# Moving elementwise steps between three engines in a five-pass graph network: low parts to GpSimd, normalisation to ScalarE, the last graph pass's own projection to ScalarE with its bias as a matmul

## Chip, cores and metric

One NeuronCore of a Trainium2 chip runs the whole program. The metric is the device time of one execution in microseconds (us); each kernel is executed several times and the median is given.

The engines are named as the profile names them: PE is TensorE's matrix unit and PEld its weight load, DVE is VectorE, ACT is ScalarE, POOL is GpSimd, SP is SyncE, which here only issues DMAs.

## What is computed

`x` holds 128 graphs of 64 nodes with 384 features, `adj` a weighted 64x64 adjacency for each. Four layers follow one another, each as `x = layernorm(x + layer(x, adj))`, all in fp32:

```
L0, L3: q, k, v = x@Wq.T, x@Wk.T, x@Wv.T + bv      (12 heads of 32)
        p = softmax(q k^T * scale + edge * adj)
        out = (p v) @ Wo.T + bo
L1:     the same with biases on q and k, beta*adj added, p masked
        where adj is 0, and no output projection
L2:     two inner layers, each
        a = softmax(h h^T / sqrt(384)); delta = a * adj
        attn = delta / (sum(delta) + 1e-10)
        ctx = (attn above diag) @ (h Wl.T + bl) + diag(attn) * (h Ws.T + bs)
              + (attn below diag) @ (h Wr.T + br)
        h = relu(layernorm(ctx) * g + b)
```

## The kernel before

The program is five passes over the same 8192 rows, one behind the other, with a barrier between them and the rows kept in device memory from pass to pass: `attention_pass` for L0 and L1, `digcn_pass` for the two inner layers of L2 (called the first and the last graph pass here), `attention_pass` for L3. The last graph pass has `ends` true: it also adds the residual and makes the outer layernorm. L0 and L3 have an output projection (`wo` true), L1 has none.

A pass treats 16 groups of 512 rows. A group is 4 units (s = 0 to 3) of 128 rows, two graphs each, so that a pass has 64 units. Every engine has its own program for a pass, written out by hand as `group(i, pair, par)`, which `over_groups` repeats; the engines meet only through semaphores, and each works through its queue strictly in order. The order of work is therefore exactly the order in which the calls stand in the five `group` functions.

**Precision by parts.** Projections multiply fp32 values as a rounded high part plus a low part. For rows, DVE turns a tile of 128x512 (`rows_turned`, L717), ACT copies it rounded into `xT[..,0,..]` (`rows_high`, L584), and the difference goes into `xT[..,1,..]` (`rows_low`): in L0 and L3 on DVE at the tail of units 2 and 3 (L723), in L1 on POOL at the tail of the same units (L372). Each projection is then 9 matmuls, in three combinations of parts. A pass does the three tiles of a group two groups ahead (attention) or one to two ahead (graph passes).

**An attention unit.** PE makes scores (L471), DVE scales them and adds the edge bias (`softmax_max`, L751), takes the row maximum (L758) and in L0 and L3 the minimum (L760). POOL subtracts the maximum (L387) and adds the bias of v for the unit (`value_bias`, L347). ACT exponentiates (L656). DVE sums (L765) and makes the reciprocal (L770 to L776). In L0 and L3 POOL adds `bo` to the residual rows (L355) and multiplies the probabilities (L398), PE transposes them (L484), the next unit but one multiplies them with v (L509), ACT and DVE split that product into parts (`oT`: L666 and `low_part`, L798), and PE makes the output projection (`output`, L524). DVE adds the residual (`residual`, L807), takes mean and variance (L811, L814), POOL makes the reciprocal root (`rstd`, L339 and L341), and DVE's `normed` writes the normalised rows (L823, one 128x384 instruction), which SP stores. In L1 POOL adds the residual (`add_rows`, L366).

Between these, PE makes the projections of the next group, ten blocks (q, k, v: L450, L444) put between the steps of the four units by the table `BETWEEN`; ACT copies each block out of PSUM (`taken`: q L598/L596, k L605/L602, v L615).

**A graph unit.** PE projects the rows left, right and self (`project`, L1165, 9 matmuls each) and, between right and self, multiplies the unit before with its attention (`context`, L1179). In unit 1 `products` (L1138) follows that, in unit 3 `attention_T` (L1149) stands behind self. ACT copies left and right out (L1242), POOL adds their biases (L1092). DVE's `itself` adds the own bias to the self projection (`hs`, L1386), `context` makes `c0 = hs * diag + ps_c` with its statistics (L1398, L1401, L1404), `inner_norm` scales, shifts, adds the residual and takes the second statistics (L1412 to L1425). In the last graph pass ACT standardises (L1259) and writes the final rows (L1267). DVE's own order in a graph unit is `itself`, `rows_turned` (L1332, units 0, 2, 3), attention steps 3 and 4 in unit 3 (L1366 to L1379: the normalised attention `wide`, which `attention_T` waits for, and `diag`), `inner_norm`, `context`, and at the tail attention step 0 (unit 1) or steps 1 and 2 (unit 2: L1352 to L1361).

## Time and profile before

| | |
|---|---|
| median of 3 executions | 2729.84 us (2726.38 to 2730.54) |
| the profiled execution, its own time | 2732.55 us |
| its span, first to last instruction | 2730.8 us |
| busy in the span: PE, DVE, POOL, ACT | 90%, 83%, 69%, 53% |
| mean granted TensorE clock | 0.966 of 2.4 GHz |
| first instruction queued by each pass: L0, L1, graph 1, graph 2, L3 | about 8, 646, 1192, 1607, 2095 us |

A row of the timeline reads: start and duration in us, engine, line, operation, output<-inputs (buffer numbers left out), shapes, xcount for merged neighbours, and in brackets the idle time ahead of it with what ended it. The windows view gives, for a stretch, the busy time of each engine with its number of instructions, then the granted clock as a share of 2.4 GHz. A busy share is an average: what bounds a stretch is read from the waits and from which engine never waits.

### The profile page before, as it was taken

To read this page: it belongs to the slowest core of one execution; us is meant where nothing else is said; L and a number is where in the kernel's file an instruction comes from. 1 tells how busy PE (TensorE), PEld (TensorE's weight loads), DVE (VectorE), ACT (ScalarE), POOL (GpSimd) and SP (SyncE) were. 2 spreads that over 40 slices of the span, in tenths; PEclk is the share of its full clock that TensorE was granted. 3 is DMA by queue.
4 is the path that set the end of the run, shared out by engine and by line. 5 is a ranking of instruction groups with operands and counts; after the bars stand their busy time and mean duration, and the time that the engine had idled before them with its cause. 6 is when DMAs were issued, how large, how long until landed. Compare 5 with 4: busy or idle time off the path is not lost. (4 is left out here: it accounts for less than half of the span.)

```text
span 2730.8 us, 64297 instructions
## 1 busy us (share of the span) xinstructions
PE 2468.6 (90%) x21490; PEld 2094.7 (77%) x21490; DVE 2263.7 (83%) x3822; ACT 1456.9 (53%) x2964; POOL 1895.4 (69%) x2093
## 2 busy tenths in 40 slices
PE   6999999995999999959999978998895999999997
PEld 5888888874877777748888867777774788888886
DVE  5999999984788888867777769889897699999997
ACT  4555555552666666535544545555554555555553
POOL 2777777773677777756666647788784577777776
PEclk9999999997999999979999989999997999999999
DMA  7222222115233332163332163333324222222211
GB/s 133 62 66 70 70 66 70 47 46 104 63 80 76 90 76 66 54 125 72 73 67 64 50 114 83 89 91 76 92 65 95 49 66 70 67 68 70 58 45 51
DMA packets 320740, 200.89 MB, mean 74 GB/s; under 512 B 243440, under 2 KB 320624, under 8 KB 320624
## 3 DMA queue, kind: packets, MB, share of 16 engines
q1 hardware_dynamic: 320624, 199.40, 31.6%
q8 instruction: 66, 1.08, 0.2%
q14 instruction: 50, 0.41, 0.0%
HBM read 136.42 MB, written 62.91 MB: 73 GB/s over the span
## 5 line engine op out<-in xcount | busy, mean ns | idle before, releaser
L450 PE MATMUL l_ps_p<-l_xT,l_w 128*128 128x512 f32 x2304 | 602.7, 409 | 99.6 <-POOL l_xT L372 50.4
L1165 PE MATMUL l_ps_h<-l_w,l_hT 128*128 128x384 f32 x3456 | 658.1, 345 | 10.1 <-DVE l_hs L1386 7.3
L1165 PEld LDWEIGHTS l_ps_h<-l_w,l_hT 128*128 128x128 f32 x3456 | 607.1, 191 | 74.0 <-issue 42.4
L450 PEld LDWEIGHTS l_ps_p<-l_xT,l_w 128*128 128x128 f32 x2304 | 430.9, 193 | 197.1 <-issue 102.2
L387 POOL TENSOR_TENSOR l_pr<-l_sc,l_st 128x768 f32<-128x768 f32 x192 | 283.1, 1475 | 328.8 <-DVE l_st L758 327.6
L347 POOL TENSOR_TENSOR v<-v,l_bvs 128x768 f32<-128x768 f32 x192 | 375.6, 1956 | 0.0
L1242 ACT ACTIVATE l_hlr<-l_ps_h 64x384 f32<-64x384 f32 x512 | 248.8, 486 | 228.3 <-PE l_ps_h L1165 219.1
L1092 POOL TENSOR_TENSOR l_hlr<-l_hlr,l_sides 128x768 f32<-128x768 f32 x128 | 240.1, 1876 | 119.9 <-ACT l_hlr L1242 119.9
L444 PE MATMUL l_ps_p<-l_w,l_xT 128*128 128x384 f32 x1584 | 311.2, 342 | 0.0
L615 ACT ACTIVATE v<-l_ps_p 64x192 f32<-64x192 f32 x704 | 228.6, 325 | 142.0 <-PE l_ps_p L444 135.3
L765 DVE TENSOR_REDUCE l_st<-l_pr 128x12 f32<-128x768 f32 x192 | 182.7, 952 | 126.9 <-ACT l_pr L656 125.7
L524 PE MATMUL l_ps_y<-l_w,l_oT 128*128 128x384 f32 x1152 | 237.6, 352 | 47.2 <-DVE l_oT L798 43.5
L444 PEld LDWEIGHTS l_ps_p<-l_w,l_xT 128*128 128x128 f32 x1584 | 273.1, 188 | 5.8 <-issue 0.2
L524 PEld LDWEIGHTS l_ps_y<-l_w,l_oT 128*128 128x128 f32 x1152 | 204.6, 193 | 80.9 <-issue 77.3
L398 POOL TENSOR_TENSOR l_pr<-l_pr,l_st 128x768 f32<-128x768 f32 x128 | 211.1, 1649 | 38.0 <-DVE l_st L776 28.6
L656 ACT ACTIVATE l_pr<-l_pr 128x768 f32<-128x768 f32 x192 | 163.1, 850 | 85.4 <-POOL l_pr L387 81.4
L751 DVE SCALAR_TENSOR_TENSOR l_sc<-l_ps_s,l_sbias 128x768 f32<-128x768 f32 x192 | 183.6, 956 | 30.1 <-PE l_ps_s L471 22.3
L651 ACT ACTIVATE l_pT<-l_ps_t 128x512 f32<-128x512 f32 (+1 forms) x384 | 167.5, 490 | 50.0 <-PE l_ps_t L484 44.4
L758 DVE TENSOR_REDUCE l_st<-l_sc 128x12 f32<-128x768 f32 x192 | 183.0, 953 | 6.7
L605 ACT ACTIVATE l_k<-l_ps_p,even_odd 128x512 f32<-128x512 f32 x192 | 121.7, 685 | 110.9 <-PE l_ps_p L450 110.9
L471 PE MATMUL l_ps_s<-l_k,l_qT 64*64 64x128 f32 x4608 | 172.1, 280 | 5.3 <-DVE l_sc L751 5.3
L484 PE MATMUL l_ps_t<-ident,l_pr 128*128 128x128 f32 x1152 | 165.5, 281 | 12.6 <-POOL l_pr L398 9.5
(127 smaller groups left out, 4297.9 us busy)
## 6 DMA issues: line engine op xcount, KB each, us to landing
rows<-l_yo SPq DMA_DIRECT2D x256, 192.0 KB, 1.9
l_xa<-rows SPq DMA_DIRECT2D x256, 192.0 KB, 4.3
l_xr<-rows SPq DMA_DIRECT2D x192, 192.0 KB, 2.4
l_xa<-in_x SPq DMA_DIRECT2D x64, 192.0 KB, 4.2
l_xr<-in_x SPq DMA_DIRECT2D x64, 192.0 KB, 2.4
out<-l_yo SPq DMA_DIRECT2D x64, 192.0 KB, 1.9
l_edge<-in_adj SPq DMA_DIRECT2D x80, 128.0 KB, 2.4
raw<-in_L_gnn_Wq SPq DMA_DIRECT2D x12, 144.0 KB, 4.8
```

The source lines that it names most:

```text
L347: nc.gpsimd.tensor_tensor(got, got, bvs[:, :, :].unsqueeze(1).to_broadcast([P, GPU, PAIRS, 64]), ALU.add).then_inc(pool_v, 1)
L387: nc.gpsimd.tensor_tensor(pr[b][:, :, :], sc[b][:, :, :], st[b][:, 0, :].unsqueeze(2).to_broadcast([P, HEADS, NODES]), ALU.subtract).then_ ...
L398: nc.gpsimd.tensor_tensor(pr[b][:, :, :], pr[b][:, :, :], st[b][:, 5, :].unsqueeze(2).to_broadcast([P, HEADS, NODES]), ALU.mult).then_inc( ...
L444: last = nc.tensor.matmul(bank[:, :D], rows[:, l, t, o * P:(o + 1) * P], W[2][:, r, t, :], start=c + t == 0, stop=c == 2 and t == KT - 1)
L450: last = nc.tensor.matmul(bank[:, :], W[m][:, l, t, o * P:(o + 1) * P], rows[:, r, t, :], start=c + t == 0, stop=c == 2 and t == KT - 1)
L524: last = nc.tensor.matmul(ps_y[:, :D], oT[b][:, l, t, :], W[3][:, r, t, :], start=c + t == 0, stop=c == 2 and t == KT - 1)
L615: i = nc.scalar.activation(v2[gpar][64 * odd:64 * odd + 64, GPU * u + g2, :, 32 * odd:32 * odd + 32], got[:, :, odd, :], ACT.Copy)
L751: nc.vector.scalar_tensor_tensor(out=sc[b][:, :, :], in0=logits[:, :, :NODES], scalar=scale, in1=sbias[par][:, s, :].unsqueeze(1).to_broad ...
L758: nc.vector.tensor_reduce(st[b][:, 0, :], sc[b][:, :, :], AX.X, ALU.max).then_inc(dve_mx, 1)
L1092: nc.gpsimd.tensor_tensor(hlr[b][:, :, :], hlr[b][:, :, :], sides[:, :, :], ALU.add).then_inc(pool_h, 1)
L1165: last = nc.tensor.matmul(ps_h[m][:, :D], hT[gpar][:, l, t, s * P:(s + 1) * P], W[m][:, r, t, :], start=c + t == 0, stop=c == 2 and t == K ...
L1242: i = nc.scalar.activation(hlr[b][half * NODES:(half + 1) * NODES, g, :], ps_h[m][g * NODES:(g + 1) * NODES, :D], ACT.Copy)
```

## The change

In all attention passes the low part of the rows is now made by POOL and stands at the head of units 2 and 3, behind `rstd` and ahead of the maximum's subtraction; DVE's `rows_low` is gone. The normalisation of all attention passes moves from DVE to ACT behind `exp`: two 128x1 instructions make minus mean and minus mean times rstd, one 128x384 instruction writes the rows. Waits on the old semaphore `dve_y` become waits on `act_y`.

```diff
@@ POOL, rows_low and group @@
 
             def rows_low(g, gpar, t):
-                if not inside(g, groups) or wo:
+                if not inside(g, groups):
                     return
                 pool.wait_ge(act_x, KT * g + t + 1)
                 nc.gpsimd.tensor_tensor(xT[gpar][:, 1, t, :], xF[:, t, :], xT[gpar][:, 0, t, :].bitcast(F32),
...
+                    for t in ((), (), (0, 1), (2,))[s]:
+                        rows_low(i + 2, par, t)
                     pool.wait_ge(dve_mx, n + 1)
                     if counted(2 * (n - 1)):
                         pool.wait_ge(pe_t, 2 * (n - 1))
@@ -390,8 +399,6 @@
                     value_bias(n, par, s)
                     if not wo:
                         add_rows(n - 2, pair * 4 + 2 * par + s // 2 - 1, b)
-                        for t in ((), (), (0, 1), (2,))[s]:
-                            rows_low(i + 2, par, t)
                         continue
                     output_bias(n - 2, pair * 4 + 2 * par + s // 2 - 1, b)
                     pool.wait_ge(dve_rinv, n + 1)
@@ ACT @@
 
+            def normed(n, count, b):
+
+                if not inside(n, units):
+                    return
+                act.wait_ge(dve_mv, n + 1)
+                nc.scalar.activation(ln[b][:, 10:11], ln[b][:, 6:7], ACT.Copy, scale=-1.0).then_inc(act_nm, 1)
+                act.wait_ge(pool_rs, n + 1)
+                act.wait_ge(act_nm, 2 * n + 1)
+                nc.scalar.activation(ln[b][:, 11:12], ln[b][:, 10:11], ACT.Copy, scale=ln[b][:, 9:10]).then_inc(act_nm, 1)
+                act.wait_ge(act_nm, 2 * n + 2)
+                if counted(16 * count):
+                    act.wait_ge(s_out[b], 16 * count)
+                nc.scalar.activation(yo[b][:, :], res[b][:, :], ACT.Identity, bias=ln[b][:, 11:12],
+                                     scale=ln[b][:, 9:10]).then_inc(act_y, 1)
+
...
+                    normed(n - 3, pair * 4 + 2 * par + (s - 3) // 2, 1 - s % 2)
                     for t in ((), (0, 1), (2,), ())[s]:
                         rows_high(i + 2, par, t)
...
+            normed(units - 3, units // 2 - 2, 1)
             values(units - 1, 1)
+            normed(units - 2, units // 2 - 1, 0)
+            normed(units - 1, units // 2 - 1, 1)
 
         @block.vector
@@ DVE, group @@
                     low_part(n - 2, s % 2)
-                    normed(n - 3, count, 1 - s % 2)
                     if s == 2:
                         edges(i + 1, pair + (1 if par else 0), 1 - par)
                     softmax_sum(n, s)
                     for t in ((0, 1), (2,), (), ())[s]:
                         rows_turned(i + 2, par, t)
-                    for t in ((), (), (0, 1), (2,))[s]:
-                        rows_low(i + 2, par, t)
 
             over_groups(dve, groups, group)
             low_part(units - 2, 0)
```

In the last graph pass (`ends`) the own bias row is split into a high row 0 and a low row 32 of a 128x384 tile `bias`, and one more matmul with `pick` (ones in rows 0 and 32, else 0) adds it in PSUM. ACT, not DVE, takes the self projection out, already multiplied with `diag`, and DVE's `c0` becomes a plain addition without a wait of its own for `diag`. DVE's unit is ordered anew: `context` at the head in the last graph pass, `rows_turned` behind `inner_norm` and `context` in both graph passes. `pick` is made once in the program's first block (a 128x128 memset and two copies of one row on DVE), `bias` in the prologue of the pass.

```diff
@@ PE, project @@
                         pe.wait_ge(dve_s, n)
-                elif counted(2 * (n - 1) + m + 1):
-                    pe.wait_ge(act_h, 2 * (n - 1) + m + 1)
+                elif counted(taken * (n - 1) + m + 1):
+                    pe.wait_ge(act_h, taken * (n - 1) + m + 1)
                 for c, (l, r) in enumerate(SPLIT):
                     for t in range(KT):
                         last = nc.tensor.matmul(ps_h[m][:, :D], hT[gpar][:, l, t, s * P:(s + 1) * P], W[m][:, r, t, :],
-                                                start=c + t == 0, stop=c == 2 and t == KT - 1)
+                                                start=c + t == 0,
+                                                stop=not (ends and m == SELF) and c == 2 and t == KT - 1)
+                if ends and m == SELF:
+                    if isinstance(n, int) and n == 0:
+                        pe.wait_ge(c_row, 2)
+                    last = nc.tensor.matmul(ps_h[m][:, :D], pick[:, :], bias[:, :], start=False, stop=True)
                 last.then_inc(pe_h, 1)
 
             def context(n, gpar, s):
@@ ACT, group @@
+                    if ends:
+                        act.wait_ge(pe_h, 3 * n + 3)
+                        act.wait_ge(dve_dg, i + 1)
+                        if counted(n - 1):
+                            act.wait_ge(dve_c, n - 1)
+                        nc.scalar.activation(hs[b][:, :], ps_h[SELF][:, :D], ACT.Copy,
+                                             scale=diag[par][:, s:s + 1]).then_inc(act_h, 1)
                     relu(n - 2, pair * 4 + 2 * par + s // 2 - 1, b)
                     if isinstance(n, int) and n == 0:
@@ DVE, context @@
                 dve.wait_ge(pe_c, n + 1)
-                dve.wait_ge(dve_s, n + 1)
-                dve.wait_ge(dve_dg, g + 1)
+                if not ends:
+                    dve.wait_ge(dve_s, n + 1)
+                    dve.wait_ge(dve_dg, g + 1)
                 if ends:
                     if counted(n - 1):
                         dve.wait_ge(act_z, n - 1)
-                nc.vector.scalar_tensor_tensor(out=c0[b][:, :], in0=hs[b][:, :], scalar=diag[gpar][:, s:s + 1],
-                                               in1=ps_c[:, :D], op0=ALU.mult, op1=ALU.add).then_inc(dve_c, 1)
+                if ends:
+                    dve.wait_ge(act_h, 3 * (n + 1))
+                    nc.vector.tensor_tensor(c0[b][:, :], ps_c[:, :D], hs[b][:, :], ALU.add).then_inc(dve_c, 1)
+                else:
+                    nc.vector.scalar_tensor_tensor(out=c0[b][:, :], in0=hs[b][:, :], scalar=diag[gpar][:, s:s + 1],
+                                                   in1=ps_c[:, :D], op0=ALU.mult, op1=ALU.add).then_inc(dve_c, 1)
                 dve.wait_ge(dve_c, n + 1)
                 nc.vector.bn_stats(ln[b][:, 0:6], c0[b][:, :]).then_inc(dve_bn, 1)
                 dve.wait_ge(s_small, 16)
@@ DVE, group @@
+                    before = (i, par, s - 1) if s else (i - 1, 1 - par, UNITS - 1)
+                    if ends:
+                        context(n - 1, *before)
                     itself(n - 1, 1 - b)
+                    if s == 3:
+                        attention(i + 1, 1 - par, 3)
+                        attention(i + 1, 1 - par, 4)
+                    if ends:
+                        inner_norm(n - 3, pair * 4 + 2 * par + (s - 3) // 2, 1 - b)
+                    else:
+                        inner_norm(n - 2, pair * 4 + 2 * par + s // 2 - 1, b)
+                        context(n - 1, *before)
                     pi[0] = pair
                     if s == 0:
                         shift_by[0] = 1
@@ -1458,17 +1511,6 @@
                     if s >= 2:
                         shift_by[0] = 2
                         rows_turned(i + 2, par, s - 2)
-                    if s == 3:
-                        attention(i + 1, 1 - par, 3)
-                        attention(i + 1, 1 - par, 4)
-                    if ends:
-                        inner_norm(n - 3, pair * 4 + 2 * par + (s - 3) // 2, 1 - b)
-                    else:
-                        inner_norm(n - 2, pair * 4 + 2 * par + s // 2 - 1, b)
-                    if s:
-                        context(n - 1, i, par, s - 1)
-                    else:
-                        context(n - 1, i - 1, 1 - par, UNITS - 1)
                     if s == 1:
                         attention(i + 1, 1 - par, 0)
                     if s == 2:
@@ DVE, behind the groups @@
+            context(units - 1, groups - 1, 1, UNITS - 1)
             if ends:
                 inner_norm(units - 3, units // 2 - 2, 1)
-            context(units - 1, groups - 1, 1, UNITS - 1)
             inner_norm(units - 2, units // 2 - 1, 0)
             inner_norm(units - 1, units // 2 - 1, 1)
 
```

How the instructions stand now on three engines; the names of tiles are l_ for any layer, the numbers are the lines of the kernel at hand.

GpSimd in the repeated groups of L0 and L3, units 2 and 3, before:

```order
L387 TENSOR_TENSOR l_pr<-l_sc,l_st 128x768
L347 TENSOR_TENSOR v<-v,l_bvs 128x768
L354 ISA
L355 TENSOR_TENSOR l_xr<-l_xr,l_bos 128x384
L398 TENSOR_TENSOR l_pr<-l_pr,l_st 128x768
L339 TENSOR_TENSOR l_ln<-l_ln,epst 128x1
L341 TENSOR_TENSOR l_ln<-l_ln,mhalf 128x1
```

and with the change (L379 is the low part, L396 the subtraction of the maximum):

```order
L346 TENSOR_TENSOR l_ln<-l_ln,epst 128x1
L348 TENSOR_TENSOR l_ln<-l_ln,mhalf 128x1
L378 ISA
L379 TENSOR_TENSOR l_xT<-l_xF,l_xT 128x512
L378 REGISTER_ALU
L379 TENSOR_TENSOR l_xT<-l_xF,l_xT 128x512
L393 REGISTER_ALU
L395 REGISTER_ALU
L396 TENSOR_TENSOR l_pr<-l_sc,l_st 128x768
```

Two low parts now stand between a unit's rstd and its subtraction in unit 2, and one in unit 3.

VectorE in the repeated groups of the last graph pass, from the tail of unit 2 into unit 3, before (L1366 and L1372 make `wide`, L1398 is `c0`):

```order
L1361 RECIPROCAL l_st<-l_st 128x4
L1385 ISA
L1386 TENSOR_TENSOR l_hs<-l_ps_h,l_own 128x384
L1330 REGISTER_ALU
L1332 STREAM_TRANSPOSE l_hF<-l_xa 128x512
L1366 TENSOR_TENSOR l_attn<-l_u,l_st 128x256
L1372 TENSOR_TENSOR l_wide<-l_attn,l_halves 128x512
L1377 TENSOR_REDUCE l_st<-l_u 128x4
L1379 TENSOR_TENSOR l_diag<-l_st 128x4
L1412 TENSOR_TENSOR l_c<-l_c,l_gain 128x384
L1414 TENSOR_TENSOR l_c<-l_c,l_shift 128x384
```

and with the change (L1397 and L1403 make `wide`, L1432 is `c0`):

```order
L1392 RECIPROCAL l_st<-l_st 128x4
L1423 REGISTER_ALU
L1431 REGISTER_ALU
L1432 TENSOR_TENSOR l_c<-l_ps_c,l_hs 128x384
L1437 BN_STATS l_ln<-l_c 128x6
L1440 BN_AGGR l_ln<-l_ln 128x2
L1397 TENSOR_TENSOR l_attn<-l_u,l_st 128x256
L1403 TENSOR_TENSOR l_wide<-l_attn,l_halves 128x512
L1408 TENSOR_REDUCE l_st<-l_u 128x4
L1410 TENSOR_TENSOR l_diag<-l_st 128x4
L1448 TENSOR_TENSOR l_c<-l_c,l_gain 128x384
```

`wide` now stands behind the `c0` of unit 2, and so behind PE's context of that unit; the transposition has moved to the unit's tail.

ScalarE in an attention unit of L0 and L3 with the change (L663 is the exponential, L605 takes q out):

```order
L663 ACTIVATE l_pr<-l_pr 128x768
L681 ACTIVATE l_ln<-l_ln 128x1
L683 ISA
L684 ACTIVATE l_ln<-l_ln 128x1
L685 REGISTER_ALU
L687 ISA
L688 ACTIVATE l_yo<-l_res,l_ln 128x384
L595 REGISTER_ALU
L605 ACTIVATE l_qT<-l_ps_p 128x512
```

Three instructions are new between the exponential and the next block that ACT takes out of PSUM.

## Rows read from the trace of the kernel before

**Rows 1.** Windows of first and last graph pass: us; PE, PEld, DVE, ACT, POOL; clock

```profile
1240.00:1600.00 360.00, 359.50 (x2541) 311.01 (x2537) 268.19 (x532) 176.63 (x359) 233.96 (x246) 1.00 0.26 61
1680.00:2040.00 360.00, 322.26 (x2198) 274.55 (x2199) 323.99 (x609) 198.14 (x357) 294.17 (x511) 0.96 0.34 83
```

**Rows 2.** Timeline of one group of L3, PE

```profile
2315.64 2.35 PE L450 MATMUL l_ps_p<-l_xT,l_w 128*128 128x512 f32 x9
...
2318.41 1.82 PE L524 MATMUL l_ps_y<-l_w,l_oT 128*128 128x384 f32 x9 [0.41 <-DVE l_oT L798]
...
2327.61 1.82 PE L524 MATMUL l_ps_y<-l_w,l_oT 128*128 128x384 f32 x9 [0.65 <-DVE l_oT L798]
```

**Rows 3.** Chain that ended last, the same wait one group later

```profile
2364.84 1.83 PE l_ps_y L524 x9
```

**Rows 4.** Timeline of the same group of L3, DVE, then POOL

```profile
2319.49 0.95 DVE L765 TENSOR_REDUCE l_st<-l_pr 128x12 f32<-128x768 f32 x1 [0.70 <-ACT l_pr L656]
...
2320.74 0.76 DVE L776 SCALAR_TENSOR_TENSOR l_st<-l_st 128x12 f32<-128x12 f32 x1
...
2326.91 0.55 DVE L798 TENSOR_TENSOR l_oT<-l_ps_o,l_oT 128x384 fp32r<-128x384 f32 x1
...
2339.61 0.17 DVE L776 SCALAR_TENSOR_TENSOR l_st<-l_st 128x12 f32<-128x12 f32 x1
2339.74 2.58 DVE L723 TENSOR_TENSOR l_xT<-l_xF,l_xT 128x512 fp32r<-128x512 f32 x2
...
2320.47 1.01 POOL L355 TENSOR_TENSOR l_xr<-l_xr,l_bos 128x384 f32<-128x384 f32 x1
```

**Rows 5.** Timeline of one group of L1: DVE from unit to unit, POOL, PE

```profile
910.95 0.96 DVE L751 SCALAR_TENSOR_TENSOR l_sc<-l_ps_s,l_sbias 128x768 f32<-128x768 f32 x1
...
918.32 0.96 DVE L751 SCALAR_TENSOR_TENSOR l_sc<-l_ps_s,l_sbias 128x768 f32<-128x768 f32 x1
...
920.43 1.48 POOL L387 TENSOR_TENSOR l_pr<-l_sc,l_st 128x768 f32<-128x768 f32 x1 [1.24 <-DVE l_st L758]
...
934.75 4.44 PE L450 MATMUL l_ps_p<-l_xT,l_w 128*128 128x512 f32 x18 [2.13 <-POOL l_xT L372]
```

**Rows 6.** PE's transposes, one a group: first pass, 14 groups apart, last, 12 apart

```profile
1229.84 0.60 PE L1149 MATMUL l_ps_a<-ident,l_wide 128*128 128x128 f32 x4
...
1575.17 0.60 PE L1149 MATMUL l_ps_a<-ident,l_wide 128*128 128x128 f32 x4
...
1673.61 0.66 PE L1149 MATMUL l_ps_a<-ident,l_wide 128*128 128x128 f32 x4 [0.27 <-DVE l_wide L1372]
...
2023.48 0.66 PE L1149 MATMUL l_ps_a<-ident,l_wide 128*128 128x128 f32 x4
```

**Rows 7.** Timeline of the last graph pass: PE, then DVE in units 2 and 3

```profile
1869.88 4.98 PE L1165 MATMUL l_ps_h<-l_w,l_hT 128*128 128x384 f32 x27
...
1868.22 0.51 DVE L1412 TENSOR_TENSOR l_c<-l_c,l_gain 128x384 f32<-128x384 f32 x1
...
1870.90 0.61 DVE L1398 SCALAR_TENSOR_TENSOR l_c<-l_hs,l_diag,l_ps_c 128x384 f32<-128x384 f32 x1
...
1872.31 0.39 DVE L1352 TENSOR_REDUCE l_st<-l_u 128x4 f32<-128x256 f32 x1
...
1875.01 0.56 DVE L1386 TENSOR_TENSOR l_hs<-l_ps_h,l_own 128x384 f32<-128x384 f32 x1
...
1876.11 0.90 DVE L1366 TENSOR_TENSOR l_attn<-l_u,l_st 128x256 f32<-128x256 f32 x1
...
1877.79 0.66 PE L1149 MATMUL l_ps_a<-ident,l_wide 128*128 128x128 f32 x4 [0.26 <-DVE l_wide L1372]
```

**Rows 8.** Three low parts at a start: DVE in L0, POOL in last graph pass

```profile
20.27 1.85 DVE L723 TENSOR_TENSOR l_xT<-l_xF,l_xT 128x512 fp32r<-128x512 f32 x3
...
1615.22 3.73 POOL L1085 TENSOR_TENSOR l_hT<-l_hF,l_hT 128x512 fp32r<-128x512 f32 x3 [6.00 <-ACT l_hT L1220]
```

**Rows 9.** Groups by line: busy us, mean ns, then idle before

```profile
L1259 ACT ACTIVATE l_c<-l_c,l_ln 128x384 f32<-128x384 f32 x64 | 45.1, 704 | 48.9 <-POOL l_ln L1076 48.7
```

75 lines of the change are left out of this document (43 added, 32 removed).

## The prediction

> **What bounds the kernel now.** I read the windows first, then the waits, then one group of each pass in the timeline on all engines, because the busy shares of the whole span (PE 90%, DVE 83%) do not say who waits for whom.
>
> The first graph pass is bound by PE: in its window PE is busy for 359.5 of 360 us, at the full 2.4 GHz [rows 1]. Its group takes (1575.17 - 1229.84)/14 = 24.67 us [rows 6]. The last graph pass does the same matmuls but takes (2023.48 - 1673.61)/12 = 29.16 us a group [rows 6]. There DVE is busy for 324 of 360 us and what is left is the short gaps between dependent instructions, so DVE's queue sets the pace. PE stands idle for 38 us of the window and its clock is 0.96 [rows 1], which is (1 - 0.96) x 2 x 360 = 29 us at 1.2 GHz.
>
> L3, and L0 with the same code, have a group of 2364.84 - 2327.61 = 37.23 us [rows 2, 3]. PE waits twice in it, 0.41 and 0.65 us, both times for DVE's low part of the attention output [rows 2]. So the most that DVE's relief can bring is 1.06 us a group. Which part of DVE's work makes PE wait matters more than how much work it has. The second wait ends a path that starts when PE finishes the first q block (2315.64 + 2.35 = 2317.99 [rows 2]): ACT copies that block out, then does exp; DVE sums (2319.49, after a wait for ACT), makes the reciprocal, turns rows, and goes through the next unit's maximum to the low part, which ends at 2326.91 + 0.55 = 2327.46 [rows 4]. `normed` and `rows_low` are not on this path. One piece on it is too long: L776, on 12 elements, takes 0.76 us from 2320.74, though it takes 0.17 at 2339.61. In the first case POOL's L355 runs from 2320.47 to 2321.48, and L776 ends with it [rows 4]: here POOL's instruction holds up DVE's.
>
> L1 shows PE waiting 2.13 us once a group for POOL's low part [rows 5]. I do not take that for its bound. DVE starts `softmax_max` at 910.95 and 918.32, 7.37 us apart [rows 5], and between them the chain goes DVE maximum, POOL subtraction, `value_bias` and `add_rows`, DVE statistics, without a pause; four such links make the group. The late low part is a result of this ring.
>
> **The change part by part.** The sum is made against the profiled execution's 2732.55 us.
>
> 1. *L0 and L3, steady.* DVE loses three low parts a group, 2.58 us for the two that stand together in unit 2 beside a busy POOL [rows 4] and about 0.6 for the third, and four normalisations. By itself this moves only the first wait (0.41): the path from the q block is untouched, and what the first wait gives back the second takes. But DVE arrives earlier at unit 0, so POOL's subtraction and with it L355 come earlier, by up to 0.8 us, which frees L776: 0.76 - 0.17 = 0.59 us off the path. Per group 0.59 us, in 14 full groups of two passes: -16.5 us. Bounds: 0 if POOL still covers L776; 2 x 14 x 1.06 = -30 if PE never waits. I take the value that the row of L776 gives. PE is then behind nothing else: the two low parts on POOL in unit 2 (3.73/3 = 1.24 us each [rows 8]) delay its exp by little, since ACT is busy with a k block and pT then.
>
> 2. *L0 and L3, start.* PE cannot begin before three low parts. DVE makes them in 1.85 us, each beside the next copy by ACT; POOL takes 3.73 [rows 8] and may begin about 0.4 earlier: +1.5 us a pass, +3 us. Bounds +0 and +3.8, the latter if nothing overlaps.
>
> 3. *Tails of three passes.* The last `normed` is on the way to the barrier. The nearest row for ACT's 128x384 instruction is 704 ns [rows 9] against some 0.5 on DVE; the two 128x1 instructions have no row. Between nothing and 704 ns each, I take 0.25 and their gaps as small: +0.7 us a pass, +2 us; bounds +0.5 and +5. The Trainium skill, "ScalarE: Activation LUTs", section What ACT_TABLE_LOAD costs, gives 186 ns plus 0.833 ns an element, and 93 ns for each per-partition pointer. By it the two small ones take 187 and 280 ns and the large one 692; the sum would be the same within 1 us. The rule also prices ACT's extra load at 1.2 us a unit, which its idle time in L0 and L3 covers.
>
> 4. *L1.* The group's ring keeps its four links. In unit 3 the one low part (1.24) just fills the 1.24 us that POOL waits ahead of its subtraction [rows 5]; in unit 2 two of them push the subtraction by 1.25 us, and DVE's sum stands there behind the edge bias anyway. PE's 2.13 us wait for the low part goes and comes back as a wait for the scores' buffer. I take +0.2 us a group, +3 us. Bounds: 2.13 x 14 = -30, if PE were the bound after all, and +1.25 x 14 = +17, if nothing hides the push.
>
> 5. *Last graph pass.* DVE loses `itself` (0.56 us [rows 7]) in each unit, PE gains one matmul, 4.98/27 = 0.184 us [rows 7]. More important is the order. `wide`, which PE's transpose in unit 3 waits for, now stands behind `context`, and `context` behind PE's own matmul for it. A new ring closes: PE's context of unit 1 starts DVE's unit 2 (context 1872.31 - 1870.90 = 1.41, `inner_norm` 1870.90 - 1868.22 = 2.68, and 1876.11 - 1872.31 = 3.80 for attention steps 1 and 2, `itself` and one transposition, less about 0.5 for `itself`: 7.4 us); then unit 3's context, 1.41, and from L1366 to the transpose 1877.79 - 1876.11 = 1.68 [rows 7]: 10.5 us with 0.1 for the first start. From the transpose round to PE's context of unit 1, PE works through its group less the piece that runs beside these 10.5: that piece is S, L, R and context of one unit and S of the next, 4 x 1.66 + 0.8 + 0.37 = 7.8 us, with 1.66 for 9 matmuls and two of the new ones. The whole group is 24.67 + 4 x 0.184 = 25.4, so 17.6 remains, at 0.96 of the clock 18.3. The ring is 28.8 us against 29.16: -0.36 us, in 14 groups -5 us. Bounds: 25.4 us a group (PE's own work), -53; and 30.1 with `inner_norm` beside POOL (1.3 us more), +13. Start of this pass: the bias's low row follows attention steps 1 to 4 and two transpositions, +0.7 us.
>
> 6. *First graph pass.* DVE's `rows_turned` moves behind `context`; PE needs the tile a unit later, and DVE is busy 268 of 360 us [rows 1]. PE's full window is the cover: 0. If it went, 0.7 us for a transposition in three units of a group would be at stake.
>
> 7. *First block.* A memset and two one-row copies ahead of DVE's memsets: +0.4 us.
>
> Sum: -16.5 + 3 + 2 + 3 - 5 + 0.7 + 0.4 = **-12.4 us**, 2732.55 to 2720.2. The median shown is 2.7 us below the profiled execution, so I forecast **2717 us**.
>
> **The rivals.** *All relief counts.* PE is busy 90% of the span and follows every relief: L0 and L3 give 30, L1 30, the last graph pass 53, less 6 at starts and tails: -107, near 2623. Against it: the order of the new ring and that of L1. That one of L1 and the last graph pass obeys it is more likely than both; that case lies at 2660 to 2695.
>
> *Nothing in L0 and L3.* POOL, with 3.7 us more a group, still covers L776, and items 2 to 7 leave +4: 2734, within 0.2%.
>
> *Slower: the new ring in the last graph pass.* PE now waits in one place, ahead of the transpose, for about 10.5 - 7.8 = 2.7 us, more than any wait there now. If the granted clock falls to 1.2 GHz for twice as much of the pass (0.92 in place of 0.96), PE's 17.6 us become 19.1 and with `inner_norm` held up by POOL the ring is 19.1 + 11.8 = 30.9, +1.7 x 14 = +24 us; with half of item 1's gain the sum is -8 + 3 + 2 + 3 + 24 + 0.7 + 0.4 = +25, 2755. It decides from 29.16 us a group on, that is once DVE's two pieces exceed 10.9 us at the present clock. For it speaks that PE's clock is below 1 in this pass alone [rows 1]; against it, that the other waits of PE there vanish. The Trainium skill, "TensorE: Matmul & The Clock Gate", section What's actually happening, says that the gate halves the array's clock after idleness; by it a single longer wait would cost more half-speed time than several short ones, which leads to this rival's 2755. The trace agrees so far that the pass with waits is the one below full clock.
>
> **How the numbers follow.** A measurement of this kernel can tell about 0.2%, 5.5 us, from no change. My forecast (2700 to 2724) has 0.42, relief beyond it 0.18, cancelling 0.18, slower by the ring or by L1's push 0.22. Range: 2686 to 2747, leaving out a tenth at each end. Faster 0.60, same 0.18, slower 0.22.
>
> **What would show it.** L0 and L3: PE's wait for `low_part` about 0.5 us a group, in one place; L776's counterpart near 0.17 in unit 0; group 36.6. L1: no wait of PE for the low part, group still 31.2 to 31.5. Last graph pass: PE waits for `wide` 2 to 3 us once a group, group 28 to 29.5. Wrong would be: L1 near 29 us a group; PE waiting for ACT's q, k or v copies; a last graph pass near 25.5 or above 30.

## The result, and the profile after

The changed kernel takes 2733.14 us (median of 20 executions, 2731.8 to 2737.14) against 2728.69 us (20 executions, 2726.38 to 2733.05): a ratio of 1.0018, 95% interval 1.0011 to 1.0024. It is 4.5 us slower, within the 0.2% that I had set as the bound, and on the other side of it than forecast (2717). The profiled execution took 2734.95 us, its span is 2733.2 us (2730.8 before).

I take the passes apart. A pass runs from its first load of an adjacency block to that of the next pass, L3 to the end of the span. A group is the time from DVE's first instruction on scores (L3, L0, L1) or on `c` (graph passes) in unit 8 to the same in unit 56, divided by 12.

| pass | us before | us after | group before | group after | group, forecast |
|---|---|---|---|---|---|
| L0 | 634.9 | 630.0 | 37.11 | 36.62 | about -0.6 |
| L1 | 542.4 | 534.9 | 31.42 | 31.12 | +0.2 |
| first graph | 415.3 | 415.4 | 24.66 | 24.66 | 0 |
| last graph | 490.7 | 512.5 | 29.04 | 30.67 | -0.36 |
| L3 | 627.8 | 620.7 | 37.24 | 36.62 | about -0.6 |

The differences are -4.9, -7.5, +0.1, +21.8 and -7.1, together +2.4 us, the difference of the two spans. So three passes became faster, and one gave back more.

The windows view of the changed kernel, for L1 and the two graph passes (columns as in [rows 1]):

```profile
670.00:1130.00 460.00, 437.80 (x4499) 361.33 (x4499) 312.11 (x474) 347.34 (x762) 344.09 (x330) 1.00 0.32 76
1228.00:1588.00 360.00, 359.24 (x2535) 310.75 (x2529) 293.52 (x532) 176.43 (x359) 231.60 (x246) 1.00 0.26 63
1673.00:2033.00 360.00, 317.80 (x2119) 273.01 (x2118) 290.25 (x529) 208.13 (x386) 281.56 (x485) 0.94 0.33 80
```

Against [rows 1], DVE in the last graph pass fell from 324 to 290 of 360 us, and yet the pass is longer: DVE now waits, PE is busy for less, and the granted clock is 0.94 of 2.4 GHz instead of 0.96. The waits of that window, longest in total first (waiting engine and line, what it waited for: us, times, longest):

```profile
PEld l_ps_a L1163 <- DVE l_wide L1403: 39.3, 11, 4.4
...
PE l_ps_a L1163 <- DVE l_wide L1403: 35.7, 11, 4.0
...
DVE l_c L1432 <- ACT l_hlr L1261: 20.9, 6, 3.5
DVE l_c L1432 <- PE l_ps_c L1198: 18.4, 23, 1.2
```

PE waits ahead of its transpose for `wide`, once a group, 3.2 us on the mean. That wait was 0.26 us in [rows 7]. The timeline of one group, PE:

```profile
1867.60 0.87 PE L1198 MATMUL l_ps_c<-l_hlr,l_aT 128*64 128x384 f32 x4
...
1880.34 1.11 PE L1163 MATMUL l_ps_a<-ident,l_wide 128*128 128x128 f32 x4 [4.03 <-DVE l_wide L1403]
1881.11 5.64 PE L1179 MATMUL l_ps_h<-l_w,l_hT 128*128 128x384 f32 x18
...
1889.32 3.29 PE L1179 MATMUL l_ps_h<-l_w,l_hT 128*128 128x384 f32 x18
...
1910.84 0.66 PE L1163 MATMUL l_ps_a<-ident,l_wide 128*128 128x128 f32 x4 [2.33 <-DVE l_wide L1403]
...
1941.76 1.11 PE L1163 MATMUL l_ps_a<-ident,l_wide 128*128 128x128 f32 x4 [4.00 <-DVE l_wide L1403]
```

And DVE between PE's context and the transpose:

```profile
1868.72 0.56 DVE L1432 TENSOR_TENSOR l_c<-l_ps_c,l_hs 128x384 f32<-128x384 f32 x1 [0.78 <-PE l_ps_c L1198]
...
1870.08 2.21 DVE L1448 TENSOR_TENSOR l_c<-l_c,l_gain 128x384 f32<-128x384 f32 x1
...
1874.53 0.71 DVE L1363 STREAM_TRANSPOSE l_hF<-l_xa 128x512 f32<-128x512 f32 x1 [0.16 <-issue]
...
1875.90 1.57 DVE L1389 SCALAR_TENSOR_TENSOR l_st<-l_st 128x4 f32<-128x4 f32 x1
...
1877.77 0.56 DVE L1432 TENSOR_TENSOR l_c<-l_ps_c,l_hs 128x384 f32<-128x384 f32 x1
...
1879.59 0.70 DVE L1403 TENSOR_TENSOR l_wide<-l_attn,l_halves 128x512 f32<-128x512 f32 x1
```

This is the ring that the prediction described: PE's context ends at 1867.60 + 0.87 = 1868.47, DVE works without a pause but for short starts, and `wide` is done at 1880.29. DVE's piece is 11.82 us in this group. Two instructions in it are long beside POOL: L1448 takes 2.21 us, 0.51 in [rows 7], and the 4-element L1389 1.57. What the 4.03-us wait costs on top stands in PE's next rows: 18 matmuls take 5.64 us after it and 3.29 a unit later. The windows view around both waits shows the clock of these stretches:

```profile
1868.50:1876.30 7.80, 7.80 (x42) 6.64 (x42) 7.04 (x12) 5.81 (x11) 7.17 (x14) 1.00 0.19 59
1879.20:1886.00 6.80, 5.66 (x19) 5.66 (x20) 4.58 (x11) 2.11 (x5) 2.96 (x8) 0.50 0.18 58
1909.00:1916.00 7.00, 4.91 (x27) 3.83 (x28) 5.18 (x12) 3.20 (x7) 3.74 (x9) 1.00 0.18 56
```

1.2 GHz from 1879.2, while PE waits, to 1886.0; full clock around the 2.33-us wait of the next group. The two kinds of group alternate (1880.34, 1910.84, 1941.76: 30.50 and 30.92 us). The other kind, PE and DVE:

```profile
1899.80 0.87 PE L1198 MATMUL l_ps_c<-l_hlr,l_aT 128*64 128x384 f32 x4
...
1902.75 2.09 DVE L1450 TENSOR_TENSOR l_c<-l_c,l_shift 128x384 f32<-128x384 f32 x1
...
1907.78 0.16 DVE L1389 SCALAR_TENSOR_TENSOR l_st<-l_st 128x4 f32<-128x4 f32 x1
...
1910.09 0.70 DVE L1403 TENSOR_TENSOR l_wide<-l_attn,l_halves 128x512 f32<-128x512 f32 x1
...
1929.04 0.87 PE L1198 MATMUL l_ps_c<-l_hlr,l_aT 128*64 128x384 f32 x4
```

Here DVE's piece is 10.12 us (1900.67 to 1910.79). `inner_norm` has a long instruction here too (L1450, 2.09) and takes 4.25 us in place of 4.45; what is shorter is above all L1389, 0.16 in place of 1.57. PE's piece, from the finished `wide` to the end of the context that starts DVE's next piece, is 20.4 us after the long wait, with the low clock in it (1880.29 to 1900.67), and 19.1 after the short one, at full clock but with 0.9 us of idle time (1910.79 to 1929.91). Over the pass the pieces are 11.0 and 19.75 us on the mean.

From unit 8 to 56 PE is idle for 3.56 us a group and busy for 27.11. In experiment 2 below, where the same matmuls run at full clock throughout, it is busy for 25.60. So the low clock, on for 3.41 us a group, costs 1.5. Before, PE is idle for 3.10 us a group and busy for 25.94, with 2.28 us at half clock. The four bias matmuls are 4 x 0.184 = 0.74. So the group's growth, 1.63 us, is 0.74 for them, 0.46 of idle time and 0.43, the rest, for the clock.

L3, one group, PE and then DVE's unit 0:

```profile
2324.69 1.82 PE L531 MATMUL l_ps_y<-l_w,l_oT 128*128 128x384 f32 x9
...
2334.08 1.82 PE L531 MATMUL l_ps_y<-l_w,l_oT 128*128 128x384 f32 x9 [0.86 <-DVE l_oT L817]
...
2327.10 0.56 DVE L789 SCALAR_TENSOR_TENSOR l_st<-l_st 128x12 f32<-128x12 f32 x1
...
2327.83 0.17 DVE L795 SCALAR_TENSOR_TENSOR l_st<-l_st 128x12 f32<-128x12 f32 x1
```

The first of the two waits of [rows 2] is gone, the second is 0.86. L795 is L776 of [rows 4]: 0.17 where it took 0.76. L789, the instruction two ahead of it, now takes 0.56.

### The profile page after: what moved, and what is told of

It reads as the page before. It is cut to its first block and busy times, and to the rows that moved or that the text cites. A ratio compares the mean times of both kernels' runs of the same rounds, so it can differ in the third digit from the quotient of the medians.

```text
span 2733.2 us, 65211 instructions
## 1 busy us (share of the span) xinstructions
PE 2471.4 (90%) x21554; PEld 2108.1 (77%) x21554; DVE 1992.3 (73%) x3475; ACT 1689.4 (62%) x3606; POOL 1969.1 (72%) x2189
## 5 line engine op out<-in xcount | busy, mean ns | idle before, releaser
L1179 PE MATMUL l_ps_h<-l_w,l_hT 128*128 128x384 f32 x3456 | 672.0, 347 | 2.3 <-issue 2.3
L1179 PEld LDWEIGHTS l_ps_h<-l_w,l_hT 128*128 128x128 f32 x3456 | 614.9, 193 | 63.3 <-issue 54.0
L396 POOL TENSOR_TENSOR l_pr<-l_sc,l_st 128x768 f32<-128x768 f32 x192 | 285.1, 1485 | 172.2 <-DVE l_st L777 172.2
L354 POOL TENSOR_TENSOR v<-v,l_bvs 128x768 f32<-128x768 f32 x192 | 356.2, 1855 | 0.0
L1106 POOL TENSOR_TENSOR l_hlr<-l_hlr,l_sides 128x768 f32<-128x768 f32 x128 | 246.7, 1928 | 125.6 <-ACT l_hlr L1261 125.4
L379 POOL TENSOR_TENSOR l_xT<-l_xF,l_xT 128x512 fp32r<-128x512 f32 x144 | 184.0, 1291 | 85.8 <-ACT l_xT L591 85.8
L405 POOL TENSOR_TENSOR l_pr<-l_pr,l_st 128x768 f32<-128x768 f32 x128 | 188.6, 1473 | 69.5 <-DVE l_st L795 69.5
L663 ACT ACTIVATE l_pr<-l_pr 128x768 f32<-128x768 f32 x192 | 162.2, 845 | 116.8 <-POOL l_pr L396 115.9
L478 PEld LDWEIGHTS l_ps_s<-l_k,l_qT 64*64 64x64 f32 x4608 | 125.7, 134 | 64.7 <-issue 58.0
```

Of the source, the lines that this page charges most:

```text
L354: nc.gpsimd.tensor_tensor(got, got, bvs[:, :, :].unsqueeze(1).to_broadcast([P, GPU, PAIRS, 64]), ALU.add).then_inc(pool_v, 1)
L396: nc.gpsimd.tensor_tensor(pr[b][:, :, :], sc[b][:, :, :], st[b][:, 0, :].unsqueeze(2).to_broadcast([P, HEADS, NODES]), ALU.subtract).then_ ...
L478: last = nc.tensor.matmul(logits[g * NODES:(g + 1) * NODES, h:h + 2, :NODES], qT[par][q, t, c:c + NODES], k2[par][q, t, :, c:c + NODES], s ...
L1106: nc.gpsimd.tensor_tensor(hlr[b][:, :, :], hlr[b][:, :, :], sides[:, :, :], ALU.add).then_inc(pool_h, 1)
L1179: last = nc.tensor.matmul(ps_h[m][:, :D], hT[gpar][:, l, t, s * P:(s + 1) * P], W[m][:, r, t, :], start=c + t == 0, stop=not (ends and m = ...
```

## The experiments

For each kernel the group times of its own profile are read as above. Ratios are against the kernel before.

**1. The attention part alone.** In place of the changed `digcn_pass` stands the one of before, so in DVE's unit:

```diff
-                    if ends:
-                        context(n - 1, *before)
                     itself(n - 1, 1 - b)
...
```

> The changed kernel's attention passes with both graph passes of the kernel before. The two profiles put the change at -4.9 us in L0, -7.5 in L1, +0.1 in the first graph pass, +21.8 in the last and -7.1 in L3. If these passes are independent, what is left is -19.5: 2709 us against 2728.7. Rival: L1's gain is not of the change (in the profile of before L1 has 0.85 us a group at half clock, and that may be one execution's luck); then only L0 and L3 gain, -12, 2717 us, and L1's group stays near 31.4.

2714.3 us, ratio 0.9945 (0.9931 to 0.9958). Groups 36.62, 31.12, 24.66, 29.07 and 36.68 us. The passes are independent of each other, L1's gain is real, and the last graph pass holds the whole loss. The profiled span is 18.5 us shorter than that of before, 19.5 expected. From here on, edits in different passes may share a kernel.

**2. DVE's old order in the last graph pass**, with the rest of the change kept:

```diff
                     if ends:
-                        context(n - 1, *before)
+                        if s == 0:
+                            shift_by[0] = 1
+                            rows_turned(i + 1, 1 - par, 2)
+                        if s >= 2:
+                            shift_by[0] = 2
+                            rows_turned(i + 2, par, s - 2)
...
                         inner_norm(n - 3, pair * 4 + 2 * par + (s - 3) // 2, 1 - b)
...
+                    context(n - 1, *before)
```

> The changed kernel, but in the last graph pass DVE's unit keeps its order of before (transposition, attention steps 3 and 4, inner_norm, context); ACT still takes the self projection out and the four bias matmuls a group stay. Theory ring: the order alone makes the loss, since `wide` stands behind `context`. With the old order the group falls below the 29.04 us of before, because DVE has 2.2 us less: 27 to 28.5 us a group, 2733 - 14 x 2.2 to 3.7 = 2681 to 2702 us. Rival work: four more matmuls and ACT's extra copy make the loss, and the order does not matter: 30.7 us a group, 2733 us.

2696.8 us, ratio 0.9879 (0.9864 to 0.9895); the group is 28.05 us. Its window:

```profile
1673.00:2033.00 360.00, 328.46 (x2277) 282.49 (x2276) 315.33 (x576) 229.40 (x421) 300.10 (x529) 1.00 0.34 84
```

Full clock, and no wait for `wide`. The order makes the loss: the ACT step and the bias matmul gain 1.0 us a group when it is left alone. Between this kernel and the changed one lie 2.62 us a group, 1.1 of them idle time of PE and 1.5 the clock. PE still idles 2.46 us a group, but in pieces, ahead of its contexts:

```profile
PE l_ps_c L1198 <- DVE l_c L1432: 18.1, 13, 1.6
PE l_ps_c L1198 <- POOL l_hlr L1106: 12.3, 19, 0.8
```

**3. The order alone**, in the kernel before (`itself` ahead of `context`, since `context` needs it):

```diff
                     itself(n - 1, 1 - b)
+                    if ends:
+                        context(n - 1, *before)
+                    if s == 3:
+                        attention(i + 1, 1 - par, 3)
+                        attention(i + 1, 1 - par, 4)
+                    if ends:
+                        inner_norm(n - 3, pair * 4 + 2 * par + (s - 3) // 2, 1 - b)
+                    else:
+                        inner_norm(n - 2, pair * 4 + 2 * par + s // 2 - 1, b)
+                        context(n - 1, *before)
                     pi[0] = pair
                     if s == 0:
...
-                    if s:
-                        context(n - 1, i, par, s - 1)
-                    else:
-                        context(n - 1, i - 1, 1 - par, UNITS - 1)
```

> The kernel before with only DVE's new order of the graph passes: in the last one `itself` then `context` at the head, in both the transposition behind inner_norm; DVE still takes the self projection out, and there is no bias matmul. With the rest of the change and the old order the last graph pass took 28.05 us a group, with all of it 30.67. Theory ring: the order alone makes the loss, and more of it, since `itself` now stands twice in DVE's piece of 11.9 us (+1.1) while PE's piece loses two bias matmuls (-0.4): 31.2 to 31.5 us a group, 2728.7 + 14 x 2.2 to 2.5 = 2759 to 2764 us. Rival: the order does harm only together with the hand-over through ACT; then 29.0 to 29.3 us a group, 2729 to 2733 us.

2753.35 us, ratio 1.0083 (1.0069 to 1.0096); the group is 30.67 us, the same as with the whole change. The order alone costs 21 us (the pass takes 511.9 us). I had expected more for `itself`. PE waits at another place here: for DVE's `hs` (L1386), which empties the PSUM block that PE's next self projection writes, 3.2 us a group, against 0.2 for `wide`. So the order makes the loss here through another step of DVE's queue than in the changed kernel:

```profile
1888.27 3.24 PE L1165 MATMUL l_ps_h<-l_w,l_hT 128*128 128x384 f32 x9 [3.46 <-DVE l_hs L1386]
```

**4. `wide` ahead of context in unit 3.**

```diff
+                    if ends and s == 3:
+                        attention(i + 1, 1 - par, 3)
+                        attention(i + 1, 1 - par, 4)
                     if ends:
                         context(n - 1, *before)
...
-                    if s == 3:
+                    if s == 3 and not ends:
```

> The changed kernel, but in unit 3 of the last graph pass attention steps 3 and 4 stand ahead of `context`. Theory ring: DVE's piece of the ring loses one context with its statistics, 1.41 us, less what step 4 adds behind it; the group goes from 30.67 to 29.3 us, 2733 - 14 x 1.4 = 2714 us, and PE's wait ahead of the transpose from 3.2 to 1.8 us a group. Rival work: no change, 2733 us.

2729.58 us, ratio 0.9993 (0.9984 to 1.0002); the group is 30.45 us. A miss: of the 1.4 us a group forecast 0.2 came, hardly more than the rival's nothing. PE's wait for `wide` fell from 3.2 to 2.6 us, not to 1.8, and a wait for the transposed tile ahead of PE's products (0.8 us a group, 0.3 in the changed kernel) took much of it back.

**5. `wide` in unit 2**, attention steps 1 to 3 right behind `context`:

```diff
                     if ends:
                         context(n - 1, *before)
+                        if s == 2:
+                            attention(i + 1, 1 - par, 1)
+                            attention(i + 1, 1 - par, 2)
+                            attention(i + 1, 1 - par, 3)
...
-                    if s == 2:
+                    if s == 2 and not ends:
```

> The changed kernel, but in the last graph pass attention steps 1 to 3 stand right behind `context` in unit 2, ahead of inner_norm and the transposition; step 4 stays in unit 3. Theory ring: from PE's context to the finished `wide` DVE now needs 1.4 + 2.5 + 1.1 = 5.0 us, less than the 7.8 us that PE has to do in that time, so PE no longer waits there, its clock stays at 2.4 GHz and the group nears PE's own work: 25.4 to 26.5 us, 2733 - 14 x 4.2 to 5.3 = 2659 to 2674 us. Rival DVE-bound: DVE's queue (290 of 360 us busy) with its gaps still sets the pace, and the group stays at 28 or more: 2696 us or above. Rival work: no change, 2733 us.

2710.62 us, ratio 0.9929 (0.9916 to 0.9943); the group is 29.23 us. The wait for `wide` is gone, as the ring theory says, but the size is that of the rival. Behind it stood the next late step, the third transposed tile:

```profile
1864.98 0.60 PE L1163 MATMUL l_ps_a<-ident,l_wide 128*128 128x128 f32 x4
...
1878.76 2.75 PE L1152 MATMUL l_ps_u<-l_hF 128*64 128x64 f32 x48 [1.91 <-DVE l_hF L1363]
```

**6. `inner_norm` last**, the transposition ahead of it, as in 5 otherwise:

```diff
+                        if s == 0:
+                            shift_by[0] = 1
+                            rows_turned(i + 1, 1 - par, 2)
+                        if s >= 2:
+                            shift_by[0] = 2
+                            rows_turned(i + 2, par, s - 2)
                         inner_norm(n - 3, pair * 4 + 2 * par + (s - 3) // 2, 1 - b)
```

> The changed kernel, but in the last graph pass DVE's unit is: context, attention steps 1 to 3 (unit 2) or 4 (unit 3), transposition, and inner_norm last. The variant with wide made in unit 2 ended PE's wait for `wide`, but PE then waited 1.9 us a group for the transposed tile behind inner_norm. Theory rings: with both ahead of inner_norm no wait is left on a ring through them, and DVE's own queue, as in the variant with the old order (28.05 us a group), is the bound: 27.3 to 28.1 us a group, 2686 to 2698 us. Rival: PE-bound at 25.5 to 26.5, 2660 to 2675 us. Rival: a further ring (inner_norm late, then ACT's and POOL's norm and the next standardised rows) keeps it at 29 or more, above 2710 us.

2704.81 us, ratio 0.9904 (0.9888 to 0.9919); the group is 28.60 us, outside each range, and slower than the old order. Each cure uncovers a wait elsewhere, here POOL's side biases behind a root that waits for the late statistics:

```profile
1893.92 0.87 PE L1198 MATMUL l_ps_c<-l_hlr,l_aT 128*64 128x384 f32 x4 [1.32 <-POOL l_hlr L1106]
```

**7. No bias matmul.** The last graph pass leaves out the own bias.

```diff
-                    last = nc.tensor.matmul(ps_h[m][:, :D], pick[:, :], bias[:, :], start=False, stop=True)
```

> The changed kernel without the four bias matmuls a group; the last graph pass leaves out the own bias. Theory ring: two of the four (units 0 and 1) stand on PE's piece of the ring, so the group loses 2 x 0.184 = 0.37 us, 30.3 us a group, 2733 - 5 = 2728 us; PE's wait for `wide` grows by the other two. Rival: all four count, 0.74 us, 29.9 us a group, 2723 us. Rival clock: with the wait unchanged and less work between, more of the pass is at half clock, and nothing is gained: 2733 us.

2724.54 us, ratio 0.9992 (0.998 to 1.0005). The eleven executions do not agree with each other: six take 2719.9 to 2724.5 us at a mean clock of 0.963 to 0.967, five 2729.3 to 2734.8 at 0.956 to 0.961. The profile is of one of the six (2723.6 us); in it the group is 29.72 us, 0.95 less, more than any of the three theories had, with 2.28 us a group at half clock instead of 3.41 and nearly the same wait for `wide` (3.0 us). The other five take about what the changed kernel takes, as the clock's rival has it. So this run tells neither what the matmuls themselves cost nor which theory holds; it shows that the same program can differ by 10 us here, together with its clock.

**8. The low parts alone**, in the kernel before:

```diff
                     rstd(n - 3, 1 - b)
+                    for t in ((), (), (0, 1), (2,))[s]:
+                        rows_low(i + 2, par, t)
```

> The kernel before with only one part of the change: the rows' low parts on POOL at the head of units 2 and 3. Theory low: this part alone makes the attention passes' gain (both parts together measured 2714.3 against 2730.2 us, -16): DVE reaches unit 0 earlier, and in L1 PE no longer waits 2.1 us for the low part. Groups 36.6 us in L0 and L3, 31.1 in L1; 2711 to 2716 us. Rival norm: DVE's normalisation is what holds the group; then this part gives little, groups stay at 37.1 and 31.4, 2727 to 2733 us. Rival both: each gives half, 2719 to 2725 us.

2718.74 us, ratio 0.9957 (0.9943 to 0.997). Groups 36.77 and 36.72 in L0 and L3, 31.47 in L1: most of the gain in L0 and L3, none in L1. None of the theories had that split. The reciprocal's small instructions in unit 0 are hardly shorter here: in L0 and L3 the first and the last take 0.90 and 0.86 us together, 0.93 before.

**9. The normalisation alone**, in the kernel before:

```diff
@@ ACT @@
+                    normed(n - 3, pair * 4 + 2 * par + (s - 3) // 2, 1 - s % 2)
@@ DVE @@
-                    normed(n - 3, count, 1 - s % 2)
```

> The kernel before with only the other part: the attention passes' normalisation on ACT, the low parts where they were. Theory low: no gain in L0 and L3, since the normalisation stands behind the low part of the attention output and is not on the path to PE's waits; L1 within 0.1 us a group; tails +1 us: 2728 to 2734 us. Rival norm: this part makes the gain, 2711 to 2716 us. Rival both: 2719 to 2725 us.

2727.41 us, ratio 0.9991 (0.9981 to 1.0). The whole hardly moves, but two large parts cancel: L0 and L3 go to 37.74 and 37.79 us a group (+0.6), L1 to 30.09 (-1.33), 521.4 us for the pass. Neither was foreseen. The timeline of L1, DVE from the start of unit 2 to that of unit 3, in the kernel before (L738 is the edge bias):

```profile
918.32 0.96 DVE L751 SCALAR_TENSOR_TENSOR l_sc<-l_ps_s,l_sbias 128x768 f32<-128x768 f32 x1
...
920.64 1.47 DVE L823 TENSOR_SCALAR l_yo<-l_res,l_ln 128x384 f32<-128x384 f32 x1
922.04 1.92 DVE L738 TENSOR_SCALAR l_off<-l_edge 128x256 f32<-128x256 f32 x1
...
926.95 0.96 DVE L751 SCALAR_TENSOR_TENSOR l_sc<-l_ps_s,l_sbias 128x768 f32<-128x768 f32 x1
```

with the normalisation alone moved:

```profile
916.71 0.96 DVE L777 SCALAR_TENSOR_TENSOR l_sc<-l_ps_s,l_sbias 128x768 f32<-128x768 f32 x1
...
919.03 1.41 DVE L764 TENSOR_SCALAR l_off<-l_edge 128x256 f32<-128x256 f32 x1
...
924.27 0.96 DVE L777 SCALAR_TENSOR_TENSOR l_sc<-l_ps_s,l_sbias 128x768 f32<-128x768 f32 x1
```

and in the changed kernel, with POOL's low parts and subtraction:

```profile
910.76 0.96 DVE L770 SCALAR_TENSOR_TENSOR l_sc<-l_ps_s,l_sbias 128x768 f32<-128x768 f32 x1
...
919.47 0.96 DVE L770 SCALAR_TENSOR_TENSOR l_sc<-l_ps_s,l_sbias 128x768 f32<-128x768 f32 x1
...
911.60 2.54 POOL L379 TENSOR_TENSOR l_xT<-l_xF,l_xT 128x512 fp32r<-128x512 f32 x2
914.09 1.53 POOL L396 TENSOR_TENSOR l_pr<-l_sc,l_st 128x768 f32<-128x768 f32 x1
```

Unit 2 takes 8.63, 7.56 and 8.71 us. In it DVE's own queue is the bound before, and `normed` is 1.47 us of that queue: its removal gives 1.07. In the changed kernel POOL makes two low parts before the subtraction, the unit is as long as before, and DVE waits in it for ACT's exponential and POOL's residual, which stand behind the subtraction. Part of L1's gain can be the clock's: before, L1 has 0.85 us a group at half clock, here and in the changed kernel none. No run tells the two apart. In L3, still with the normalisation alone moved, the first of the reciprocal's small instructions is long in units 3 and 0:

```profile
2335.93 1.02 DVE L796 SCALAR_TENSOR_TENSOR l_st<-l_st 128x12 f32<-128x12 f32 x1
```

In [rows 4] the one long instruction there is L776, 0.76 us. Over unit 8 to 56 the first and last of these instructions take 1.20 us together in units 0, 1 and 3, 0.93 before, and PE's waits for `low_part` grow by 0.3 to 0.4 us a group. Another 0.3 is PE waiting for POOL's multiplied probabilities (L405), for which it waited 0.01 before. So the +0.6 is waiting of PE; what makes those steps late is argued from the rows and not isolated by a run.

**10. Low parts of L1 back at the tail; POOL's side biases first.** DVE's old order in the last graph pass as in 2.

```diff
-                    for t in ((), (), (0, 1), (2,))[s]:
+                    for t in ((), (), (0, 1), (2,))[s] if wo else ():
                         rows_low(i + 2, par, t)
...
                         add_rows(n - 2, pair * 4 + 2 * par + s // 2 - 1, b)
+                        for t in ((), (), (0, 1), (2,))[s]:
+                            rows_low(i + 2, par, t)
...
                     if ends:
+                        side_biases(n, s % 2)
                         rstd(n - 4, s % 2, epst, 17, dve_mv2, pool_ve2, pool_rs2)
```

> The changed kernel with three edits in separate passes. L1: the low parts go back to the tail of POOL's units 2 and 3, where they were. Last graph pass: DVE's old order, as in the variant with the old order (28.05 us a group), and POOL adds the side biases ahead of the reciprocal root of the unit four before. L1, theory: with the normalisation alone moved, L1 took 30.09 us a group against 31.12 with both parts; its unit 2 is 7.56 us against 8.72, so the low parts at the head cost 1.15 us a group, and at the tail L1 takes 30.1 again, 521 us in place of 535. Rival: other contention, no gain. Last graph pass, theory: PE's waits ahead of its context (2.4 us a group) are partly POOL's side biases waiting behind the root, so 27.3 to 27.8 us a group; rival: DVE's queue is the bound, 28.05 stays. Whole: 2696.8 - 14 - 0 to 10 = 2673 to 2683 us; without L1's gain 2687 to 2697.

2719.71 us, ratio 0.996 (0.9947 to 0.9974). L1: 30.17 us a group, 522.9 for the pass, as the theory has it. Last graph pass: 30.22 in place of 28.05, a miss; now the roots are late, ACT waits for them, and PE for ACT's copy of the self projection (2.3 us a group, none in experiment 2).

**11. The same with `inner_norm` last**, that is experiment 6 with both edits of 10:

```diff
+                        side_biases(n, s % 2)
                         rstd(n - 4, s % 2, epst, 17, dve_mv2, pool_ve2, pool_rs2)
```

> The same two edits in L1 and on POOL, but in the last graph pass DVE has inner_norm last (the variant that took 28.60 us a group, with 3.0 us of PE waiting for POOL's side biases, which waited for inner_norm's statistics). Theory: the ring PE context, DVE context and inner_norm, POOL root, POOL side biases, PE context is cut, and PE's waits of 3.0 us go: 25.8 to 26.8 us a group, 2704.8 - 14 - 25 to 39 = 2652 to 2666 us. Rival: DVE's own queue (314 of 360 us busy) keeps it at 27.5 to 28.6: 2676 to 2691 us.

2740.24 us, ratio 1.0037 (1.0023 to 1.005); 31.61 us a group, 4.1 us of it PE's wait behind ACT's copy. The same miss, larger.

**12. All low parts at the tail of POOL's units**, with DVE's old order in the last graph pass:

```diff
                     rstd(n - 3, 1 - b)
-                    for t in ((), (), (0, 1), (2,))[s]:
-                        rows_low(i + 2, par, t)
```

> The changed kernel with the low parts of all attention passes at the tail of POOL's units 2 and 3, and DVE's old order in the last graph pass. L1 should take 30.1 us a group as above. L0 and L3, theory that only DVE's relief counts: 36.6 us a group at the tail as at the head, 2683 us. Rival that POOL's place counts: at the head they delay the subtraction and spare `p` a wait, at the tail they delay nothing that PE waits for, 36.2 or less, 2677 us or less; or they hold up the small instructions of the reciprocal on DVE, 37 or more, 2690 us or more.

2683.37 us, ratio **0.983** (0.9817 to 0.9843): 1.7% faster than before, and the best of all. Groups 36.63, 30.17, 24.66, 28.04, 36.63. In L0 and L3 head or tail is the same to 0.01 us, though the small instructions of the reciprocal take 3.5 us a group at the tail and 4.4 at the head. Those of unit 0 did not change with the place of the low parts (the row at 2311.78, against 0.56 at 2327.10 above); those of the later units did, and the group stayed as it was:

```profile
2311.78 0.62 DVE L791 SCALAR_TENSOR_TENSOR l_st<-l_st 128x12 f32<-128x12 f32 x1
...
2330.53 0.20 DVE L791 SCALAR_TENSOR_TENSOR l_st<-l_st 128x12 f32<-128x12 f32 x1
```

## Why the prediction was wrong, step by step

**Item 5, the last graph pass, failed: -5 forecast (and +0.7 for its start), +21.8 measured.** The mechanism was found, the sizes of both pieces of the ring were not. PE's piece was put at 17.6 us, "at 0.96 of the clock 18.3"; it is 19.75 on the mean. DVE's piece was put at 10.5; it is 11.0 on the mean, 11.8 and 10.1 in turn. Together 30.7 us in place of 28.8. In PE's piece the low clock was taken from a kernel with short waits: after the long wait it comes to 20.4 us, and after the short one to 19.1, where PE waits again for a transposed tile, 0.6 us of 0.9, which the sum had at nothing. In DVE's piece `inner_norm` takes 4.45 or 4.25 us for the 2.68 of [rows 7], because in each group one of its 128x384 products stands beside POOL (2.21 or 2.09 in place of 0.5); I took it from rows that did not meet a POOL instruction. Against that, from L1397 to the finished `wide` are 1.2 us, priced at 1.68, and attention steps with the transposition take 3.2 us when L1389 is long and 1.8 when it is not, priced at 3.3 from a group in which it was long.

The rival with the slower ring had 11.8 and 19.1 us and +24. Its direction was right and I gave it too little weight, but that its total nearly fits is in part luck: 11.8 belongs to the groups with the long wait and 19.1 to the others, and the clock is 0.94, not 0.92. What spoke for it was misread too: the clock was below 1 not in this pass alone, L1 also had 0.85 us a group at half. Experiments 2 and 3 show the step itself: in the kernel before the order costs 21 us alone, and the other part of the item gains 17 us (490.7 to 473.4).

**Item 4, L1, failed in sign: +3 forecast, -7.5 measured**, 4 of it in the repeated groups. The low parts at the head do push the subtraction, as item 4 says, and alone they change the group by +0.05 us (experiment 8). What was left out is `normed`. It was counted as work off DVE in items 1 and 3, but never as 1.47 us in unit 2 of L1, where the queue of DVE was the bound. Alone it gives 1.33 us a group (experiment 9); at the head the low parts take 1.0 of it back, at the tail almost nothing (experiments 10 and 12). The statement that the ring alone sets L1's pace held for three units and not for the fourth. That PE's wait for the low part is a result and not the bound was right: it went, and waits of 1.24 us a group for the copy of v and 0.5 for the scores' buffer took its place. The wait for a copy by ACT was one of the prediction's own signs of being wrong.

**Items 1 to 3, L0 and L3: the number came out, the mechanism did not. -11.5 forecast** (-16.5 + 3 + 2, the 2 being for three tails), **-12.0 measured.** The group fell by 0.49 and 0.62 us for 0.59, and one of PE's two waits for `low_part` is gone. But the gain was to come from L776. Its counterpart is at 0.17 as foretold; L789, two instructions ahead, went up to 0.59 on the mean, so unit 0's pair went from 0.93 us to 0.76, 0.17 and not 0.59 less. With the low parts alone it lost 0.03 and 0.07 us, and the groups fell by 0.34 and 0.52 all the same (experiment 8). Nor did PE's waits for `low_part` fall by 0.59: from 0.95 and 1.11 us a group in two pieces to 0.90 in one, where 0.5 was forecast. Most of the gain, 0.36 us a group, is in PE's busy time (36.1 to 35.74). It is 36.1 in both kernels where PE waits twice a group (before, experiment 9) and 35.7 in those where it waits once (8, 12 and the changed one). So losing one wait saved more than its idle time; why, no run shows. That the sum fits is luck. And `normed`, held to be off the path, is not: alone it makes L0 and L3 slower by 0.6 us a group, and with the low parts moved it is worth 0.1. The starts are within what profiles of equal code differ by (the time from the first edge load to unit 8 is 97.8 to 100.1 us in L3 for the same code), so +1.5 can't be confirmed. ACT's three instructions of `normed` take 0.20, 0.29 and 0.71 us, as priced.

**Items 6 and 7** held: the first graph pass differs by 0.1 us, and nothing else shows.

**The sum.** Forecast -12.4, measured +2.4 in the spans. Item 5 was off by 26 us, item 4 by -10.5: the time lies inside the range only because two errors cancelled in part.
